# Cross-attention on one Trainium2 core: queries and keys made transposed for two batches at once, probabilities turned through DRAM and VectorE

## The reference

```python
# layer 0, per batch, C = 128, T = 512
Mn = Wn @ inorm(x_c) + bn;  Mm = Wm @ inorm(x_s) + bm
A  = softmax(einsum('bct,bcs->bts', Mn, Mm), -1)          # 512 x 512
Ml = Wl @ x_s + bl
x  = Wo @ einsum('bcs,bts->bct', Ml, A) + bo + x_c
# layer 1, 128 rows, D = 512, H = 16 heads of 32
n = layer_norm(x, ln1)
q = n @ q_w + q_b;  k = ctx @ k_w + k_b;  v = ctx @ v_w + v_b
attn = softmax(where(mask, q k^T / sqrt(32), -max), -1)   # per head 128 x 128
hidden = (attn v) @ cproj_w + cproj_b + x
out = hidden + gelu(layer_norm(hidden, ln2) @ fc_w + fc_b) @ proj_w + proj_b   # 512 -> 2048 -> 512
```

## Time and profile before

| what | value |
|---|---|
| median of 3 runs | 3121.52 us (3120.23 to 3122.07) |
| profiled execution: own time, span | 3121.42 us, 3119.6 us |
| mean granted PE clock, share of full | 0.994 |
| PE busy | 3067.8 us, 98%, 18551 instructions |
| PEld (weight loads) busy | 2558.2 us, 82% |
| DVE, ACT, POOL busy | 1950.8 (63%), 1350.4 (43%), 817.7 us (26%) |
| DMA | 147.54 MB, mean 47 GB/s |

### The profile page before, as it was taken

The page is one execution under the profiler, slowest core; times in us unless marked ns, Lnnn a source line. Parts: engine busy times, 40 slices in busy tenths (PEclk is TensorE's granted clock), DMA queues, the critical chain, the costliest instruction groups (busy, mean ns, idle before and its releaser), DMA issues. The chain is left out here.

```text
span 3119.6 us, 54886 instructions
## 1 busy us (share of the span) xinstructions
PE 3067.8 (98%) x18551; PEld 2558.2 (82%) x18551; DVE 1950.8 (63%) x3961; ACT 1350.4 (43%) x3954; POOL 817.7 (26%) x742
## 2 busy tenths in 40 slices
PE   7999999999999999999997999999999999999999
PEld 5888888888888888888886788888888888888887
DVE  7888888888888888888885533333333333333332
ACT  4666666666666666666665211111111111111111
POOL 4444444444444444444443100000000000000000
PEclk9999999999999999999998999999999999999999
DMA  4111111111111111111112211111111111111110
GB/s 121 46 51 50 50 51 53 52 55 53 52 50 50 50 50 50 50 50 50 50 38 73 92 32 41 41 40 40 40 32 22 40 33 34 40 40 40 40 27 14
DMA packets 231920, 147.54 MB, mean 47 GB/s; under 512 B 142912, under 2 KB 176192, under 8 KB 231872
## 3 DMA queue, kind: packets, MB, share of 16 engines
q1 hardware_dynamic: 231872, 146.91, 15.9%
HBM read 97.57 MB, written 33.55 MB: 42 GB/s over the span
## 5 line engine op out<-in xcount | busy, mean ns | idle before, releaser
L1173 ACT ACTIVATE gl<-pre,fc_bias 128x512 f32<-128x512 f32 x256 | 176.6, 690 | 1119.4 <-PE pre L1258 1119.4
L1212 DVE CAST hT_hi<-gl 128x512 fp32r<-128x512 f32 x256 | 109.1, 426 | 837.7 <-ACT gl L1173 837.7
L627 ACT ACTIVATE rows<-bank,negmax 128x128 f32<-128x128 f32 x1024 | 362.9, 404 | 89.5 <-DVE negmax L808 89.5
L1256 PE MATMUL pre<-yT_lo,rest_hi 128*128 128x512 f32 x768 | 298.8, 389 | 0.0
L1257 PE MATMUL pre<-yT_hi,rest_lo 128*128 128x512 f32 x768 | 298.8, 389 | 0.0
L1258 PE MATMUL pre<-yT_hi,rest_hi 128*128 128x512 f32 x768 | 298.8, 389 | 0.0
L1256 PE MATMUL acc<-rest_lo,hT_hi 128*128 128x512 f32 x768 | 298.8, 389 | 0.0
L1257 PE MATMUL acc<-rest_hi,hT_lo 128*128 128x512 f32 x768 | 298.8, 389 | 0.0
L1258 PE MATMUL acc<-rest_hi,hT_hi 128*128 128x512 f32 x768 | 298.8, 389 | 0.0
L517 POOL TENSOR_TENSOR rows<-rows,rsum 128x512 f32<-128x512 f32 x256 | 259.0, 1043 | 18.7 <-DVE rsum L702 18.7
L872 PEld LDWEIGHTS bank<-ident,rows 128*128 128x128 f32 x2048 | 232.6, 141 | 21.3 <-ACT rows L627 3.7
(11 more groups left out here) (158 smaller groups left out, 7322.6 us busy)
## 6 DMA issues: line engine op xcount, KB each, us to landing
x_in<-in_x SPq DMA_DIRECT2D x64, 256.0 KB, 2.6
ctx_in<-in_ctx SPq DMA_DIRECT2D x64, 256.0 KB, 2.9
blocks<-in_ctx SPq DMA_DIRECT2D x256, 64.0 KB, 1.9
small<-in_x SPq DMA_DIRECT2D x64, 256.0 KB, 3.3
hidden<-hid SPq DMA_DIRECT2D x64, 256.0 KB, 2.0
rows<-hidden SPq DMA_DIRECT2D x16, 1024.0 KB, 5.4
out<-rows SPq DMA_DIRECT2D x64, 256.0 KB, 2.0
stage<-y SPq DMA_DIRECT2D x240, 64.0 KB, 2.1
```

Source lines behind the costliest of these rows:

```text
L627: act.activation(probs[:, r, c, :], by_chunk(S1_BANK[r])[:, c, :], ACT.Exp, bias=negmax1[:, r, c:c + 1], accum_out=sum1[:, r, c:c + 1]).th ...
L1173: act.activation(gl[:, i % 2, :], pre[i % 2][:], ACT.Gelu_apprx_tanh, bias=mlp.fc_bias[:, i:i + 1]).then_inc(gelu_done, 1)
L1256: pe.matmul(out, a_hi, b_lo, start=first, stop=False)
```

## The change

1. **q and k for two batches at once, already transposed.** `project_pair` holds slices of the weights stationary (128 x 128) and moves 256 columns, 128 of each of two batches, so that the result is q^T or k^T. It makes half of the 512 output rows per call (`qk(0)`, `qk(1)`). Keys are made in even slots, queries in odd ones. The PE transposes of q and k go, and so do the two copies on ACT; the bias of the first half is added by ACT, of the second by DVE.
2. **Probabilities turned without PE.** SP writes them to a DRAM tensor `p_turn` (four DMAs of 256 KB, rows of 32 floats) and reads them back to `p_blocks` (four DMAs, rows of 512 floats); DVE turns 32 x 32 blocks into `pT`, four instructions of 128 x 512. The 16 transposes on PE and the four copies on ACT go.
3. **Six batches in flight.** The masked scores are of batch s-3, PV and C of batch s-5; the loop holds four slots (`Batch.period`), LAST is B+4.
4. **Moved between engines**: scaling of A and the upper halves of the normalised inputs go from DVE to ACT. x, ctx and `hid` have one buffer instead of two, x1b and v four instead of two; raw weights are loaded to buffers of their own; banks are dealt anew.
5. **MLP's PE loop** is over single groups.

```diff
@@ PE
-            def project(out, hi, lo, weight, done, chunks=range(DC)):
+            def project_pair(out, hi, lo, weight, half, done):
+                for i in range(2):
+                    cols = slice((2 * half + i) * P, (2 * half + i + 1) * P)
+                    for c in range(DC):
+                        last = three_passes(out[:, i * 2 * P:(i + 1) * 2 * P], weight_hi(weight, c)[:, cols],
+                                            weight_lo(weight, c)[:, cols],
+                                            hi[:, c, :, :].rearrange("p u n -> p (u n)"),
+                                            lo[:, c, :, :].rearrange("p u n -> p (u n)"), c == 0, c == DC - 1)
+                last.then_inc(done, 1)
...
-                        turn(bank[PT_BANK[r]], lambda c: probs[:, r, c, :], pT_turned)
-                    turn(bank[QT_BANK], lambda c: q_sb[:, c * P:(c + 1) * P], qT_turned)
-                    turn(bank[KT_BANK], lambda c: k_sb[:, c * P:(c + 1) * P], kT_turned)
+                qk(0)
...
+                qk(1)
...
+                    pe.wait_ge(u_lo_set, b1.nth(1, 1))
+                    three_passes(bank[OUT0_BANK][:], small_hi[:, 2, :], small_lo[:, 2, :], u_hi[:], u_lo[:])\
+                        .then_inc(out0_done, 1)
...
-            groups(pe, group)
+            group(Item(0, 0, G))
+            with pe.Fori(0, G - 2) as turn_:
+                group(Single(turn_, 1, G))
+            group(Item(0, G - 1, G))
@@ SP
+            def write_probs(e):
+                if e.has_before(1):
+                    after(pT_set, (e + -1).nth(4, 4))
+                after(probs_set, e.nth(4, 4))
+                for d in range(4):
+                    sp.dma_start(p_turn[d].rearrange("p (h b) -> p h b", b=32),
+                                 mlp.rows[:, 1, :, :].rearrange("p r (c d b) -> p d (r c) b", d=4, b=32)[:, d])\
+                      .then_inc(p_written, 16)
+            def read_probs(e):
+                after(p_written, e.nth(64, 64))
+                for d in range(4):
+                    sp.dma_start(p_blocks[32 * d:32 * (d + 1), :, :],
+                                 p_turn[d].rearrange("(q p) n -> p q n", p=32)).then_inc(p_blocks_in, 16)
@@ DVE
+                def turn_probs(r):
+                    if b4.exists():
+                        dve.transpose(pT[:, r, :, :].rearrange("p c (q b) -> p c q b", b=32),
+                                      p_blocks[:, :, r * P:(r + 1) * P].rearrange("p q (c b) -> p c q b", b=32))\
+                           .then_inc(pT_set, 1)
...
-                    for t in range(DC):
-                        dve.tensor_scalar(A[:, t, :], A[:, t, :], rsum0[:, t:t + 1], None,
-                                          ALU.mult).then_inc(a_scaled, 1)
...
+                if b4.exists():
+                    dve.wait_ge(p_blocks_in, b4.nth(64, 64))
+                for r in range(4):
+                    turn_probs(r)
+                if b1.exists():
+                    dve.wait_ge(u_hi_set, b1.nth(1, 1))
+                    lower(u_lo[:], bank[U_BANK][:], u_hi[:], u_lo_set)
@@ ACT
+                    for t in range(DC):
+                        act.activation(A[:, t, :], A[:, t, :], ACT.Identity,
+                                       scale=rsum0[:, t:t + 1]).then_inc(a_scaled, 1)
...
                 if b3.exists():
+                    if b4.exists():
+                        act.wait_ge(p_written, b4.nth(64, 64))
                     for r in range(4):
...
                             act.activation(probs[:, r, c, :], by_chunk(S1_BANK[r])[:, c, :], ACT.Exp,
```

More of the change, by code:

```diff
@@ L256, in attention_pass @@
         vecs_in = sem("vecs_in")
-        stage_in = [sem(f"stage_in{i}") for i in range(2)]
+        raw_w_in = [sem(f"raw_w_in{i}") for i in range(4)]
         consts_set = sem("consts_set")
@@ L331, in attention_pass @@
         probs_set = sem("probs_set")
-        pT_turned = sem("pT_turned")
-        pT_copied = sem("pT_copied")
+        p_written = sem("p_written")
+        p_blocks_in = sem("p_blocks_in")
+        pT_set = sem("pT_set")
         outT_done = sem("outT_done")
@@ L376, in slots, with pair_half @@
                     ahead[s]()
-                slot(Item(0, s, B))
-            with eng.Fori(0, PAIRS) as pair:
-                for s in range(LOOPED, LOOPED + 2):
-                    slot(Item(pair, s, B))
-            for s in range(LOOPED + 2 * PAIRS, LAST + 1):
+                slot(Batch(0, s, B))
+            with eng.Fori(0, TURNS) as turn:
+                for s in range(LOOPED, LOOPED + Batch.period):
+                    slot(Batch(turn, s, B))
+            for s in range(LOOPED + Batch.period * TURNS, LAST + 1):
                 if ahead and s in ahead:
                     ahead[s]()
-                slot(Item(0, s, B))
+                slot(Batch(0, s, B))
         def flat(t):
             return t[:].rearrange("p c n -> p (c n)")
+        def pair_half(t, e):
+            return t[:, :, e.parity, :]
         def by_chunk(b):
@@ L462, in slot @@
                     sp.dma_start(x_res, x[e.number]).then_inc(x_res_loaded, 16)
+                e = s + -2
+                if e.exists():
                     u = e.parity
@@ L469, in slot @@
                                  mask[e.number].partition_broadcast(4)).then_inc(mask_loaded[u], 16)
-                if (s + -1).first():
-                    stage_weight(C_W)
+                if s.first():
+                    load_weight(C_W)
+                e = s + -5
+                if e.exists():
+                    after(hid_set, e.nth(1, 1))
+                    sp.dma_start(hidden[e.number], hid[:]).then_inc(hid_stored[e.parity], 16)
+                if (s + -4).exists():
+                    read_probs(s + -4)
                 e = s + 1
@@ L474, in slot @@
                     load_blocks(e)
+                e = s + 2
+                if e.exists() and e.has_before(2):
+                    load(e)
             def load_for_mlp():
-                sp.wait_ge(w_hi_set, 16)
-                for i in range(4):
-                    sp.wait_ge(w_lo_set[i], 4)
                 for u in range(2):
@@ L513, in slot, with normalise @@
                 b0, b1, b2, b3, ahead = s, s + -1, s + -2, s + -3, s + 1
-                if b3.exists():
-                    for r in range(4):
+                def normalise(r):
+                    if b3.exists():
                         pool.wait_ge(rsum1_set, b3.nth(4, r + 1))
@@ new lines, in maxima1 @@
+                def maxima1(r):
+                    if b3.exists():
+                        dve.tensor_reduce(negmax1[:, r, :], by_chunk(S1_BANK[r]), AX_X, ALU.max,
+                                          negate=True).then_inc(max1_set, 1)
+                if b5.exists():
+                    dve.wait_ge(outT_hi_set, b5.nth(1, 1))
+                    lower(flat(outT_lo), bank[PV_BANK][:], flat(outT_hi), outT_lo_set)
+                if b5.exists() and not b4.exists():
+                    first_group()
@@ L873, in turn, with project @@
                 last.then_inc(done, 1)
-            def project(out, hi, lo, weight, done, chunks=range(DC)):
-                for c in chunks:
+            def project(out, hi, lo, weight, done):
+                for c in range(DC):
                     last = three_passes(out[:], hi[:, c, :], lo[:, c, :], weight_hi(weight, c),
                                         weight_lo(weight, c), c == 0, c == DC - 1)
-                if c == DC - 1:
-                    last.then_inc(done, 1)
-            def slot(s):
-                b0, b1, b2, b3, b4 = s, s + -1, s + -2, s + -3, s + -4
+                last.then_inc(done, 1)
@@ L1289, in _, with group @@
                 turn(Item(0, 0, G), c)
-            def group(g, first):
+            def group(g):
                 for i in range(IC):
```

608 lines of the change are left out of this document (298 added, 310 removed).

## The result

The changed kernel takes 3274.9 us (median of 4 runs, 3272.1 to 3276.7) against 3121.6 us before: ratio 1.049, 95% interval 1.047 to 1.051. The forecast was 3058 us with a range from 3010 to 3250. Its sign was wrong, and the time lies above the range.

A forecast was written before the change was run, and what follows sets the result against it. PE's own work was taken as the bound. Some 60 full slots, each 1.62 us shorter (25.76 to 24.14), give 97 us less, the ends 33 more: from 3121.5 to 3058 us, range 3010 to 3250.

The forecast's parts named there:

- What bounds the kernel: Kernel before: PE's own work sets both attention and MLP; PE busy 98% of the span, DVE next in attention.
- PE's part: PE's work per attention slot falls from 25.76 to 23.14 us: transposes go, 256-column products take 0.117 us each.
- What waits next: In attention, PE waits 1.0 us per slot (0.3 to 1.6) at out0 for DVE's u_lo; slot 24.14 us.
- The bounce: Probabilities out to DRAM and back: a loop of 23.4 us, 0.7 below the slot, so costed at nothing.
- The 12.5 us before the DMA: Loop's part on DVE and POOL, such as turns, maxima and normalisations: 12.2 us, with handovers 12.5.
- The write: 1 MB of probabilities to DRAM in 128-byte pieces at 205 GB/s: 6.9 us, costing slot time from 7.6.
- The read: 1 MB back from DRAM in 2 KB pieces: four issues, the last landing 2.6 us after its own, 4.0 us.
- Ends: First and last attention slots: one more, thinner slot is paid, 33 us taken between 17 and 37.
- MLP loop: Seven more edges of the MLP's PE loop cost nothing, covered by PE's queue; otherwise up to 1 us each.
- Rival 1: The write to DRAM becomes the bound in attention from 7.6 us on; up to 3322 us; chance 0.30.
- Rivals 2 and 3: Attention, second: no stall at out0, 2998 us, chance 0.10; third: weight loads stop hiding, 3208 us, chance 0.05.

The follow-up runs named there:

- e1_no_bounce: Changed kernel with both bounce DMAs left out, DVE turning the probabilities where POOL left them (another output): 3063.9 us.
- e2_write_2k: Changed kernel with the write to p_turn in 2 KB pieces instead of 128 bytes (another output): 3083.4 us.
- e9_before_mlp1: Kernel before the change, with only the MLP's PE loop over single groups: 3121.6 us, ratio 0.9998.
- e3_v_first: Changed kernel with the value product v in front of out0 on PE: 3267.7 us.
- e4: Changed kernel with DVE's wait for p_blocks and turns at the end of its slot, PV and C later on PE: 3401.5 us, ratio 1.090 against before.
- e5: Changed kernel with DVE's wait for p_blocks and turns moved from before u_lo to before v's bias: 3149.0 us, ratio 1.009 against before.
- e10: Changed kernel with DVE's turns before v's bias and PE's PV behind the transposes of A: 3126.1 us, ratio 1.001 against before.
- e11: e10 with sixteen direct SBUF to SBUF DMAs in place of the way through DRAM: 3123.9 us, ratio 1.0007 against before.
- e13: Changed kernel with direct SBUF copy, turns split, PV behind A's first transposes, a quarter of v before out0: 3084.0 us, ratio 0.988 against before.
- e14: Changed kernel with each read DMA of p_turn filling 128 partitions instead of 32 (another output): 3235.8 us.
- e8_direct: Changed kernel with sixteen 64 KB DMAs copying probabilities from SBUF to SBUF in place of the way through DRAM: 3107.6 us.
- e15_read_0213: Changed kernel with the four reads of p_turn in the order 0, 2, 1, 3: 3261.4 us.

## Why the prediction was wrong

Point by point, in its own order.

- **What bounds the kernel: right**, and **PE's part: nearly right.** Products of 256 columns start 0.12 us apart (0.117 taken). PE's work per slot is 23.6 us where 23.14 had been worked out (e1_no_bounce).
- **What waits next: right.** out0 waits for `u_lo` 0.8 us per slot where the bounce is absent (1.0 taken, 0.3 to 1.6). Work and wait together make 24.38 us for 24.14.
- **The bounce: here it failed**, in the two DMA terms of the loop. The 12.5 us before the DMA came out to a tenth: 12.53. The write was put at 6.9 us and takes 8.0. The read was put at 4.0 us and takes 6.7. Loop 27.2 instead of 23.4, and with it the slot, by medians of the three distances.
  - *The write* was mis-sized in its rate: 205 GB/s, read off the peaks of single copies of 64 KB, is only where it begins; the megabyte ends at 174. SP's issue was not counted as longer either, but four issues of 2048 pieces each take 4.33 us, where four of the other loads took 1.88.
  - *The read* was mis-sized by a wrong row. It was built from three issues and the landing of a single load of 256 KB (2.6 us), with the rate of stores (348 to 492 GB/s) as proof that a megabyte fits in that time. A store is not a load into 32 partitions, and the page of before has a load of the right size, of 1024 KB, that lands 5.4 us after issue (the row below). With 5.4 the loop is 24.8 and no longer hidden, though by itself that would still have been a gain. This was the larger error, 2.7 of 3.8 us, and the piece that had no bound above it: the prediction took both ends for the write and none for the read.

```profile
rows<-hidden SPq DMA_DIRECT2D x16, 1024.0 KB, 5.4
```

- **Ends: too small.** 33 us were taken beside 60 full slots. 63 came beside the loop's 55; with 60 slots at 1.6 us each, 55 are left. Without the bounce the difference beside the 55 slots is 18 us: e1's span is 57.5 us shorter than that of before, and its loop 1416.8 - 1341.1 = 75.7. So some 45 us are the bounce once more, in the first and last slots. Behind the loop PE waits 26.3 us for the turns, in e1 5.3, and the granted clock is low there (0.68 from 1800 to 1900 us). A shorter bounce costs less at the ends: e2_write_2k, with e1's slot, takes 19.5 us more than e1.
- **MLP loop: right**, nothing (e9_before_mlp1).
- **Rivals.** Rival 1 it was, by its place (turns waiting for `p_blocks`, `u_lo` queued behind them, PE in front of out0) and by its sign; but its price was worked out for the write alone. With a write of 8.0 us and a read of 4.0 the loop would have been 24.5 us, a slot still shorter than before. The measured time lies in the upper half of its price, up to 3322 us, which the range left out by choice; that it lies inside that price at all is luck, for the read carried it there. Rivals 2 and 3 fall: out0 does wait, and weight loads hide behind 256 columns.

What the two traces did not settle by themselves, the runs did: the low clock and the stall look like the cause on PE's rows, but filling the stall (e3_v_first) gains nothing, while shorter writing alone (e2_write_2k) brings the slot to that of the run without bounce.

## What to carry to other kernels

A transfer that is "off the path" still closes a loop if its result is queued, on an in-order engine, ahead of what feeds the next transfer: write the loop down engine by engine, and give both bounds to each DMA in it, the read as well as the write. Take a DMA's time from a row with the same direction, bytes, piece size and partitions, not from a rate of another kind. When a loop is cut, look for the next wait by the list of waits before counting the gain: four runs here gave less than their arithmetic (e4, e5, e10, e11), and the one that came nearest had put work in front of every wait (e13).

## What had not been expected

- **Issuing took longer with more pieces.** Four DMAs of 256 KB keep SP for 4.33 us in pieces of 128 bytes (2048 pieces each) and for 1.81 us in pieces of 2 KB (128 each).
- **The number of partitions that one DMA fills matters by nearly a factor of two.** Pieces of 2 KB: 410 GB/s for a load into 128 partitions and 307 to 430 for e14's, some 220 for loads that fill 32 each.
- **The low clock came behind some waits and not behind others.** With one wait of 0.8 us per slot in front of out0 (e1_no_bounce), or one of 1.3 (e8_direct), the granted clock stayed at 1.00. Behind 1.9 us v ran at the low level, and behind 2.8 us out0 too, which put x1 into the loop and made the way from the turns to the write 0.7 us longer (e15_read_0213). The length of one wait does not decide it alone: in e3_v_first waits of some 0.9 and 1.1 us, one soon behind the other, came with a clock of 0.96.
